# Masking causal scores in a grouped attention: a mask matmul on TensorE against an addition on VectorE

## The chip, the cores and the metric

The kernel runs on 1 core of one Trainium2 chip. The metric is device time in microseconds, shown as the median of 3 runs. Instructions run on five engines that each work through their own queue in order: PE (TensorE, matmuls; PEld are its weight loads), ACT (ScalarE), DVE (VectorE), POOL (GpSimd) and SP (SyncE, which issues DMAs). They are held together by semaphores: an instruction adds to one when it is done (`then_inc`), and an engine waits for a value (`wait_ge`).

## The reference

The program is four layers of attention and feed-forward on x of 8 batches x 128 tokens x 256 features. The change is in the last one, a grouped-query attention with a causal mask: 16 query heads of 128, 4 key and value heads.

```python
    h = rmsnorm(hidden, attn_norm_w)
    q = (h @ q_w.T).reshape(B, S, Hq, hd)
    k = (h @ k_w.T).reshape(B, S, Hkv, hd)
    v = (h @ v_w.T).reshape(B, S, Hkv, hd)
    q = rmsnorm(q, q_norm_w).transpose(0, 2, 1, 3)
    k = rmsnorm(k, k_norm_w).transpose(0, 2, 1, 3)
    ...
    q = apply_rope(q, cos, sin)
    k = apply_rope(k, cos, sin)
    k = jnp.repeat(k, n_rep, axis=1)
    v = jnp.repeat(v, n_rep, axis=1)
    scores = jnp.einsum('bhqd,bhkd->bhqk', q, k) * scale
    causal = jnp.tril(jnp.ones((S, S), bool))
    scores = jnp.where(causal[None, None], scores, jnp.finfo(scores.dtype).min)
    attn = jnp.einsum('bhqk,bhkd->bhqd', jax.nn.softmax(scores, axis=-1), v)
    attn = attn.transpose(0, 2, 1, 3).reshape(B, S, Hq * hd)
    hidden = hidden + attn @ o_w.T
```

## The kernel before

Stages follow one another on every engine; the grouped attention is the second half of `s47_pe`, `s47_act`, `s47_dve` and `s47_pool`, from about 895 to 1166 us. Its loop runs over m = 0 to 31: m = 4b + g, batch b and group g, a group being one key head and its four query heads. All tiles are float32 with 128 partitions (the tokens), four heads of 128 side by side (128x512, one bank of PSUM).

The order of work is written out by hand in each engine's loop over m, several groups being under way at once. In iteration m:

- PE (lines 2040 to 2068): `scores(m+1)`, `queries(m+3)` (projection, line 1916), `turn_probs(m)` (transposes, line 1922), `output(m-1)` (line 1967), `turn_queries(m+2)` (line 1922), then by g: 0 the keys of the next batch (line 1897), 2 the turning of those keys (`turn_keys`, line 1922), 3 the values (line 1904); last `weigh(m)` (probabilities by values, line 1958).
- ACT (lines 2228 to 2245): `copy_probs(m)` (line 2184), `exps(m+1)` (line 2175, four activations, each with an accumulator read; the scale is a pointer to the queries' norm, the bias a pointer to minus the maximum times that norm), `query_squares(m+3)` (line 2143), `copy_queries(m+2)` (line 2168); by g: 0 the squares of the last batch's output (line 2189) and of the next keys, 2 the copy of the turned keys (line 2164).
- DVE (lines 2515 to 2536): `copy_out(m-1)` (line 2458), at g = 0 the copy of the values (line 2439), `maxima(m+1)` (maximum, line 2443, and bias, line 2447), at g = 1 `normalise` (line 2470), `rotate_queries(m+3)` (lines 2403, 2405, 2419), `divide(m+1)` (lines 2451 and 2453), at g = 0 `hidden` (lines 2464 and 2466). At g = 2 it does `rotate_keys` (lines 2403, 2405, 2427, 2432) and the division ahead of the rotation of the queries.
- POOL raises the sums of squares to the power -1/2 (lines 2560 and 2564).

In the first iterations the engines also finish the last batches of the low-rank layer and of the memory attention (the parts `first`, `second`, `third`, `early`, `middle`, `late`).

The scores of two groups lie in the PSUM banks 4 and 2 in turn. The causal mask is 0 or -1e30, read from DRAM to `h_ca` (128x128); `tables` (lines 2290 to 2298, run once at m = 9 of the loop before) copies it four times side by side into `h_cm` as bfloat16. PE starts each group's scores with the identity times that mask and adds the four heads' products on top:

```python
pe.matmul(P[:, bank, :], idb[:, :], h_cm.rearrange("p j t -> p (j t)"), start=True, stop=False)   # line 1942
```

The maximum (DVE) and the exponentials (ACT) both read the masked scores in PSUM; PE may write a bank again when the exponentials of the group two before have ended (`h_exp`, line 1941).

Of the kernel before, what the change touches and what calls it, by code (L numbers as in the profile page):

```python
# [21 lines left out]
BF16 = mybir.dt.bfloat16  # L22
# [3 lines left out]
ALU = mybir.AluOpType  # L26
ACT = mybir.ActivationFunctionType
AX = mybir.AxisListType

B, T, D = 8, 128, 256  # L30
# [41 lines left out]
def build(nc, x, ctx, ctxT, mask, maskT, kvmask, a_wqT, a_wkT, a_wvT, a_bq, a_bk, a_bv, a_sel,  # L72
# [5 lines left out]
    with ex:  # L78
        def sb(name, shape, dt=F32):
            return ex.enter_context(nc.sbuf_tensor(name, shape, dt))  # L80
# [4 lines left out]
        P = ex.enter_context(nc.psum_tensor("P", [128, 8, 512], F32))  # L85
# [7 lines left out]
        idb = sb("idb", [128, 128], BF16)  # L93
# [1545 lines left out]
        fr2 = Arena(big2)  # L1639

        def heads3(at):
            return big3[:, at:at + 512].rearrange("p (j t) -> p j t", j=4)
# [27 lines left out]
        h_an, h_fn = fr2.view([128, D]), fr2.view([128, D])  # L1670
        h_qw, h_kw, h_c, h_sn, h_ca = (fr2.view([128, 128]) for _ in range(5))
        h_Cq, h_Sq, h_Ck, h_Sk = (fr2.view([128, 128]) for _ in range(4))
        h_cm = fr2.view([128, 4, T], BF16)
        H2 = [fr2.view([128, D]) for _ in range(2)]
        h_hh = fr2.view([128, D])
        h_V = [fr2.view([128, 512]) for _ in range(2)]
# [2 lines left out]
        h_qTs, h_kr, h_kTs, h_pts, h_t1, h_t2, h_jq, h_jk = map(  # L1679
            heads3, (0, 512, 1024, 1536, 7424, 7936, 8448, 8960))  # L1680
        h_pr = [heads3(9472), heads3(9984)]
        h_ss, h_sv, h_sr = (sm.view([128, B]) for _ in range(3))
        h_qs, h_qv, h_rq = (sm.view([128, 4, 4]) for _ in range(3))
        h_ks, h_kv, h_rk = (sm.view([128, 4]) for _ in range(3))
        h_mx, h_bi, h_z, h_r = ([sm.view([128, 4]) for _ in range(2)] for _ in range(4))
# [10 lines left out]
        h_qss, h_kss, h_qT, h_kT, h_exp, h_PT, h_yss, i_lgT, i_sl, h_s0 = act_again = (  # L1696
            a_e, c_ss, c_qkT, c_exp, c_PT, d_h, b_lgT, b_cTs, b_h, a_ab)
        h_v0, h_r0, h_qve, h_rqs, h_kve, h_rks, h_yve, h_yrs, i_cc = pool_again = (
            a_qkf, a_vp, a_p, a_parts, a_cc, c_cb, c_ve, c_rs, a_rt)
        h_ld, h_ld2, h_lt, i_ld, i_z = map(sem, ("h_ld", "h_ld2", "h_lt", "i_ld", "i_z"))  # L1700
        CLEAR = 6

        def again(eng, sems):
# [58 lines left out]
        def s47_pe(pe, last_rows):  # L1762
# [172 lines left out]
            def scores(m):  # L1935
                bank = 4 - 2 * (m % 2)
                pe.wait_ge(h_qT, m + 1)
                if m % 4 == 0:
                    pe.wait_ge(h_kT, m // 4 + 1)
                if m >= 2:  # L1940
                    pe.wait_ge(h_exp, m - 1)
                pe.matmul(P[:, bank, :], idb[:, :], h_cm.rearrange("p j t -> p (j t)"), start=True, stop=False)
                for j in range(4):
                    t = pe.matmul(P[:, bank, j * T:j * T + T], h_qTs[:, j, :], h_kTs[:, m % 4, :], start=False,
                                  stop=(j == 3))
                t.then_inc(h_s, 1)

            def turn_probs(m):
# [83 lines left out]
                    turn_fed()  # L2032
                weigh4(m)
            pe.wait_ge(e_exp, NM)
            pe.wait_ge(h_tab, 2)
            scores(0)
            turn_queries(1)
            pe.wait_ge(h_ld2, 64)
            queries(2)
            for m in range(NM):  # L2040
                b, g = divmod(m, 4)
                if m + 1 < NM:
                    if m == 0:
                        pe.wait_ge(e_vs, NM)
                    scores(m + 1)
                if m + 3 < NM:
                    queries(m + 3)
                first(NM + m)
                if m == 0:
                    pe.wait_ge(e_oT, NM)  # L2050
                turn_probs(m)
                second(NM + m)
                if m == 0:
                    output4(LAST)
                if m == 1:
                    pe.wait_ge(e_x, B)
                if m > 0:
                    output(m - 1)
                if m + 2 < NM:
                    turn_queries(m + 2)  # L2060
                if b + 1 < B and g == 0:
                    keys(b + 1)
                if b + 1 < B and g == 2:
                    turn_keys(b + 1)
                if b + 1 < B and g == 3:
                    values(b + 1)
                third(NM + m)
                weigh(m)
            output(NM - 1)

        def s47_act(act, last_rows):
# [98 lines left out]
            def exps(m):  # L2170
                act.wait_ge(h_bias, m + 1)
                if m >= 2:
                    act.wait_ge(h_t, m - 1)
                for j in range(4):
                    t = act.activation(h_pr[m % 2][:, j, :], P[:, 4 - 2 * (m % 2), j * T:j * T + T], ACT.Exp,  # L2175
                                       bias=h_bi[m % 2][:, j:j + 1], scale=h_rq[:, m % 4, j:j + 1],
                                       accum_out=h_z[m % 2][:, j:j + 1])
                t.then_inc(h_exp, 1)
# [17 lines left out]
            for m in range(NM):  # L2196
# [22 lines left out]
                if m == 4:  # L2219
                    act.wait_ge(tb_pe, 4 * B)  # L2220
                    for i in range(B - FED):
                        act.activation(XNT[:, :, (FED + i) * T:(FED + i) * T + T],
                                       P[:, 6, i * D:i * D + D].rearrange("p (k t) -> p k t", k=KD),
                                       ACT.Copy).then_inc(tb_ev, 1)
            exps(0)
            copy_queries(1)
            query_squares(2)
            for m in range(NM):
                b, g = divmod(m, 4)
                exps_memory(NM + m)  # L2230
                copy_probs(m)
                if m + 1 < NM:
                    exps(m + 1)
                first(NM + m)
                second(NM + m)
                if m + 3 < NM:
                    query_squares(m + 3)
                if m + 2 < NM:
                    copy_queries(m + 2)
                if b > 0 and g == 0:  # L2240
                    out_squares(b - 1)
                if b + 1 < B and g == 0:
                    key_squares(b + 1)
                if b + 1 < B and g == 2:
                    copy_keys(b + 1)
            out_squares(B - 1)

        def s47_dve(dve, last_rows):
# [40 lines left out]

            def tables():  # L2290
                dve.wait_ge(h_lt, 112)
                dve.tensor_copy(h_cm, h_ca.rearrange("p (a t) -> p a t", a=1).broadcast_to([128, 4, T])).then_inc(h_tab, 1)
                for C, S, w in ((h_Cq, h_Sq, h_qw), (h_Ck, h_Sk, h_kw)):
                    dve.tensor_tensor(C, h_c, w, ALU.mult)
                    dve.tensor_tensor(S[:, 0:64], h_sn[:, 0:64], w[:, 64:128], ALU.mult)
                    t = dve.tensor_tensor(S[:, 64:128], h_sn[:, 64:128], w[:, 0:64], ALU.mult)
                t.then_inc(h_tab, 1)
                dve.wait_ge(h_tab, 2)

            def choose(b):  # L2300
                n = 9 * b
# [138 lines left out]

            def maxima(m):
                dve.wait_ge(h_s, m + 1)
                dve.tensor_reduce(h_mx[m % 2], P[:, 4 - 2 * (m % 2), :].rearrange("p (j t) -> p j t", j=4), AX.X,
                                  ALU.max, negate=True).then_inc(h_max, 1)
                dve.wait_ge(h_max, m + 1)
                dve.wait_ge(h_rqs, m + 1)
                dve.tensor_tensor(h_bi[m % 2], h_mx[m % 2], h_rq[:, m % 4, :], ALU.mult).then_inc(h_bias, 1)
# [32 lines left out]
            for m in range(NM):  # L2480
# [20 lines left out]
                if m == CLEAR + 3:  # L2501
                    tables()
# [7 lines left out]
                late(m)  # L2510
            copy_out4(LAST)
            maxima(0)
            divide(0)
            rotate_queries(2)
            for m in range(NM):
                b, g = divmod(m, 4)
                if m > 0:
                    copy_out(m - 1)
                if b > 0 and g == 0:
                    copy_values(b)  # L2520
                if m + 1 < NM:
                    maxima(m + 1)
                early(NM + m)
                if b > 0 and g == 1:
                    normalise(b - 1)
                if b + 1 < B and g == 2:
                    rotate_keys(b + 1)
                    divide(m + 1)
                if m + 3 < NM:
                    rotate_queries(m + 3)  # L2530
                if m + 1 < NM and not (b + 1 < B and g == 2):
                    divide(m + 1)
                middle(NM + m)
                if b > 0 and g == 0:
                    hidden(b - 1)
                late(NM + m)
# [344 lines left out]
        @block.tensor  # L2881
        def _(pe):
            s0_pe(pe)
            s1_pe(pe)
            s47_pe(pe, s23_pe(pe))
            s8_pe(pe)
# [75 lines left out]
```

## Time and profile before

| | us |
|---|---|
| Runs: median (lowest, highest) of 3 | 1280.46 (1277.91, 1283.02) |
| The profiled execution: its time | 1279.11 |
| The profiled execution: its span in the trace | 1277.3 |
| Busy over the span: PE, DVE, ACT, POOL | 1087.5, 705.4, 503.4, 319.8 |

The profile is one execution. A page gives busy times and the chain of work that ended last, followed back from the last instruction to what released each one. Windows give each engine's busy time in a stretch with the number of its instructions, and the granted clock of TensorE (1.00 is 2.4 GHz, 0.50 is 1.2 GHz). A timeline lists instructions in order: start, duration, engine, line, operation, output<-input, shape, count, and in brackets how long the engine stood idle before and what released it. Starts follow one another closer than the durations, since an engine begins an instruction while the last one is ending. All times in the trace count from the start of the span. Some matmul records are missing (16 of 32 of line 1942).

### The profile page before, as it was taken

Reading aid. Unit: us, or ns where it says so; the run is one execution under the profiler, and the core shown is the slowest. Engines: PE = TensorE matmul, PEld = TensorE weight load, DVE = VectorE, ACT = ScalarE, POOL = GpSimd, SP = SyncE. Lnnn points to the kernel's source line nnn. Section 1 sums busy time; section 2 is a strip of 40 time slices with the busy share of each in tenths; the row PEclk is TensorE's granted clock in tenths of the full one; section 3 lists DMA queues with packets and bytes.
Section 4 is the critical chain, followed back from the end, with each engine's and each line's share of the span. In section 5 each row is a group of like instructions: output and inputs, shape, how many; then the busy total and the mean of one; then the engine's idle time right before and its main releaser. Section 6 shows DMA issues by size and latency. Waiting matters only on the chain.

```text
span 1277.3 us, 20613 instructions
## 1 busy us (share of the span) xinstructions
PE 1087.5 (85%) x7154; PEld 835.0 (65%) x7170; DVE 705.4 (55%) x1700; ACT 503.4 (39%) x1785; POOL 319.8 (25%) x440
## 2 busy tenths in 40 slices
PE   1788887899997688889999999997779999997494
PEld 0354545789996456678888888885556666665373
DVE  5876766211222778864454555555566666663544
ACT  0154563233231456654333333332445555553121
POOL 5543310222322345520000000001121222220472
PEclk9998996799999699999999999998989999998697
DMA  6443305898884070000000000032000000000595
GB/s 190 118 134 96 102 28 166 308 327 322 314 327 153 2 264 2 2 28 2 19 1 1 1 1 1 1 100 66 1 1 5 5 5 5 5 5 12 170 318 191
DMA packets 59732, 121.31 MB, mean 95 GB/s; under 512 B 9050, under 2 KB 37482, under 8 KB 53714
## 3 DMA queue, kind: packets, MB, share of 16 engines
q1 hardware_dynamic: 52217, 106.62, 24.9%
q0 software_dynamic: 4416, 12.06, 2.8%
q10 hardware_dynamic: 2996, 1.32, 0.4%
q8 instruction: 58, 0.95, 0.3%
q14 instruction: 45, 0.36, 0.1%
HBM read 107.29 MB, written 12.49 MB: 94 GB/s over the span
## 4 chain that ended last, share of the span: by engine, by line
PE 61%; DVE 17%; issue 7%; ACT 6%; DMA 6%; POOL 2%; SPq 1%; ACTq 0%; DVEq 0%; POOLq 0%
PE P L856 6%; PE P L866 5%; PE P L1778 4%; PE P L1771 4%; PE P L1823 4%; PE P L1787 4%; ACT big L2175 3%; DVE small L480 2%; PE P L1916 2%; PE P L2694 2%; PE P L1796 2%; PE P L1811 2%; DMA big<-b_w 2%; PE P L1922 2%; PE P L341 2%
## 5 line engine op out<-in xcount | busy, mean ns | idle before, releaser
L139 POOL TENSOR_TENSOR lrs<-lve,mhalf 128x1 f32<-128x1 f32 x64 | 36.6, 573 | 366.0 <-DVE lve L130 333.9
L480 DVE TENSOR_REDUCE small<-P 128x2 f32<-128x512 f32 x128 | 83.6, 681 | 44.4 <-PE P L305 43.8
L895 ACT ACTIVATE big<-P,big 128x128 f32<-128x128 f32 x184 | 52.5, 368 | 127.4 <-PE P L856 127.4
L2086 ACT ACTIVATE big<-P,small 128x128 f32<-128x128 f32 x128 | 45.3, 366 | 145.1 <-DVE small L2264 145.1
L556 ACT ACTIVATE big<-P 128x512 f32<-128x512 f32 x128 | 72.0, 598 | 64.0 <-PE P L323 58.3
L856 PE MATMUL P<-big 128*128 128x128 f32 x736 | 89.0, 281 | 1.7 <-DMA big<-b_w 1.5
L856 PEld LDWEIGHTS P<-big 128*128 128x128 f32 x736 | 86.6, 197 | 3.0 <-DMA big<-b_w 2.6
L305 PE MATMUL P<-big 90*128 90x256 bf16 x256 | 56.2, 310 | 32.3 <-DMA big<-scr_qk 17.5
L866 PE MATMUL P<-big 128*128 128x256 f32 x368 | 83.1, 380 | 0.0
L2255 DVE COPY big<-P 128x512 f32<-128x512 f32 x32 | 22.1, 692 | 107.2 <-PE P L1787 107.2
L988 DVE COPY big<-P 128x256 f32<-128x256 f32 x23 | 9.8, 425 | 127.5 <-PE P L866 127.5
L2403 DVE TENSOR_TENSOR big<-P,big 128x512 f32<-128x512 f32 x40 | 27.6, 690 | 85.4 <-ACT big L2143 85.2
L866 PEld LDWEIGHTS P<-big 128*128 128x128 f32 x368 | 68.4, 191 | 8.2
L1967 PE MATMUL P<-big 128*128 128x256 f32 x256 | 63.7, 394 | 0.8 <-DVE big L2458 0.8
L1771 PE MATMUL P<-XNT,big 128*128 128x128 f32 x512 | 62.6, 276 | 0.0
L1778 PE MATMUL P<-CT,big 128*128 128x128 f32 x512 | 62.4, 275 | 0.0
L1916 PE MATMUL P<-big,XNT 128*128 128x512 f32 x128 | 61.4, 603 | 1.2 <-DVE big L2405 1.2
L305 PEld LDWEIGHTS P<-big 90*128 90x128 bf16 x256 | 20.9, 105 | 62.7 <-DVE small L480 29.2
L1922 PEld LDWEIGHTS P<-idf,big 128*128 128x128 f32 x288 | 35.4, 146 | 40.0 <-issue 22.9
L1823 PE MATMUL P<-big 128*128 128x256 f32 x256 | 60.6, 380 | 0.0
L1787 PE MATMUL P<-big,CT 128*128 128x512 f32 x128 | 60.2, 593 | 0.0
L1771 PEld LDWEIGHTS P<-XNT,big 128*128 128x128 f32 x512 | 59.7, 192 | 0.2 <-issue 0.2
(383 smaller groups left out, 2590.6 us busy)
## 6 DMA issues: line engine op xcount, KB each, us to landing
big<-b_w SPq DMA_DIRECT2D x23, 1028.0 KB
big<-b_w SPq DMA_DIRECT2D x23, 1024.0 KB
big<-scr_qk SPq DMA_DIRECT2D x96, 96.0 KB
big<-i_wgu SPq DMA_DIRECT2D x23, 352.0 KB
big<-moe_y SPq DMA_DIRECT2D x16, 256.0 KB, 4.2
big<-i_wd SPq DMA_DIRECT2D x23, 176.0 KB
scr_qk<-big SPq DMA_DIRECT2D x8, 384.0 KB
moe_x<-XN SPq DMA_DIRECT2D x16, 128.0 KB, 1.8
```

The costliest lines, as they stand in the source:

```text
L305: t = pe.matmul(P[:, h % 2, c * D:c * D + D], QS[n % 3][0:90, h, c * 128:c * 128 + 128], KS[n % 3][0:90, h, :], start=True, stop=True)
L480: dve.tensor_reduce(negM[:, h, :], P[:, h % 2, :].rearrange("p (c s) -> p c s", c=2), AX.X, ALU.max, negate=True).then_inc(a_max, 1)
L556: act.activation(ER[:, g % 8], P[:, second_bank(i), :].rearrange("p (c t) -> p c t", c=2), ACT.Exp).then_inc(a_e, 1)
L856: m = pe.matmul(P[:, 2 * (j % 2) + f // 4, f % 4 * 128:f % 4 * 128 + 128], w1x[j % 3][:, k * F0 + f * 128:k * F0 + f * 128 + 128], xgT[j % ...
L866: m = pe.matmul(P[:, 6 + j % 2, 0:D], hT[j % 2][:, f, :], w2x[j % 3][:, f, :], start=(f == 0), stop=(f == FC - 1))
L1771: pe.matmul(P[:, 0, j * T:j * T + T], e_wqk[:, g, 0, k, j * 128:j * 128 + 128], XNT[:, k, b * T:b * T + T], start=(k == 0), stop=(k == KD ...
L1778: t = pe.matmul(P[:, 1, j * T:j * T + T], e_wqk[:, g, 1, k, j * 128:j * 128 + 128], CT[:, k, b * T:b * T + T], start=(k == 0), stop=(k == ...
L1787: t = pe.matmul(P[:, 2, :], CT[:, k, b * T:b * T + T], e_wvs[:, g, k, :], start=(k == 0), stop=(k == KD - 1))
L1823: t = pe.matmul(P[:, 7, 0:D], e_o[:, j, :], e_wos[:, 4 * g + j, :], start=(g == 0 and j == 0), stop=(g == 3 and j == 3))
L1916: t = pe.matmul(P[:, 0, :], XNT[:, k, b * T:b * T + T], h_wqs[:, g, k, :], start=(k == 0), stop=(k == KD - 1))
L1922: t = pe.transpose(P[:, bank, j * T:j * T + T], src[:, j, :], idf[:, :])
L1967: t = pe.matmul(P[:, 7, 0:D], h_o[:, j, :], h_wos[:, 4 * g + j, :], start=(g == 0 and j == 0), stop=(g == 3 and j == 3))
```

## The change

The mask matmul goes; the score matmuls each write their own quarter of the bank (`start=True`). DVE adds `h_ca`, broadcast over the four heads, while it takes the scores from PSUM to a new SBUF tile `h_sm` (two of them, in the place of the queries and keys of the attention before), waits for that to end, and takes the maximum from `h_sm`. The exponentials read `h_sm`. PE may write a bank again when DVE's masking of the group two before is done (`h_sma`); DVE may write an `h_sm` again when the exponentials of two before have ended. The bfloat16 copy of the mask and PE's wait for it go.

```diff
-        h_cm = fr2.view([128, 4, T], BF16)
+        h_sm = [heads3(2304), heads3(2816)]
...
@@ scores (PE)
                 if m >= 2:
-                    pe.wait_ge(h_exp, m - 1)
-                pe.matmul(P[:, bank, :], idb[:, :], h_cm.rearrange("p j t -> p (j t)"), start=True, stop=False)
+                    pe.wait_ge(h_sma, m - 1)
                 for j in range(4):
-                    t = pe.matmul(P[:, bank, j * T:j * T + T], h_qTs[:, j, :], h_kTs[:, m % 4, :], start=False,
-                                  stop=(j == 3))
+                    t = pe.matmul(P[:, bank, j * T:j * T + T], h_qTs[:, j, :], h_kTs[:, m % 4, :], start=True,
+                                  stop=True)
...
             pe.wait_ge(e_exp, NM)
-            pe.wait_ge(h_tab, 2)
             scores(0)
@@ exps (ACT)
-                    t = act.activation(h_pr[m % 2][:, j, :], P[:, 4 - 2 * (m % 2), j * T:j * T + T], ACT.Exp,
+                    t = act.activation(h_pr[m % 2][:, j, :], h_sm[m % 2][:, j, :], ACT.Exp,
@@ tables (DVE)
-                dve.tensor_copy(h_cm, h_ca.rearrange("p (a t) -> p a t", a=1).broadcast_to([128, 4, T])).then_inc(h_tab, 1)
...
-                dve.wait_ge(h_tab, 2)
+                dve.wait_ge(h_tab, 1)
@@ maxima (DVE)
                 dve.wait_ge(h_s, m + 1)
-                dve.tensor_reduce(h_mx[m % 2], P[:, 4 - 2 * (m % 2), :].rearrange("p (j t) -> p j t", j=4), AX.X,
-                                  ALU.max, negate=True).then_inc(h_max, 1)
+                if m >= 2:
+                    dve.wait_ge(h_exp, m - 1)
+                dve.tensor_tensor(h_sm[m % 2], P[:, 4 - 2 * (m % 2), :].rearrange("p (j t) -> p j t", j=4),
+                                  h_ca.rearrange("p (a t) -> p a t", a=1).broadcast_to([128, 4, T]),
+                                  ALU.add).then_inc(h_sma, 1)
+                dve.wait_ge(h_sma, m + 1)
+                dve.tensor_reduce(h_mx[m % 2], h_sm[m % 2], AX.X, ALU.max, negate=True).then_inc(h_max, 1)
```

## Rows read from the trace of the kernel before

**Rows 1.** The page, its part on the chain of work that ended last, by engine.

```profile
PE 61%; DVE 17%; issue 7%; ACT 6%; DMA 6%; POOL 2%; SPq 1%; ACTq 0%; DVEq 0%; POOLq 0%
```

**Rows 2.** Window of the whole stage: length, busy us by engine, clock, DMA share, GB/s.

```profile
895.00:1166.00 271.00, 237.06 (x1070) 156.85 (x1086) 174.15 (x397) 140.65 (x653) 57.41 (x97) 0.98 0.01 4
```

**Rows 3.** Timeline of PE, batches in the middle of the stage.

```profile
1007.15 1.05 PE L1944 MATMUL P<-big 128*128 128x128 f32 x8 [0.39 <-issue]
...
1071.48 1.05 PE L1944 MATMUL P<-big 128*128 128x128 f32 x8 [0.39 <-issue]
...
1079.27 0.38 PE L1942 MATMUL P<-big,idb 128*128 128x512 bf16 x1
1079.48 1.05 PE L1944 MATMUL P<-big 128*128 128x128 f32 x8
1080.38 1.88 PE L1916 MATMUL P<-big,XNT 128*128 128x512 f32 x4
1082.10 0.60 PE L1922 MATMUL P<-idf,big 128*128 128x128 f32 x4
...
1101.73 0.66 PE L1922 MATMUL P<-idf,big 128*128 128x128 f32 x4 [0.64 <-DVE big L2432]
...
1135.82 1.05 PE L1944 MATMUL P<-big 128*128 128x128 f32 x8 [0.40 <-issue]
```

**Rows 4.** Timeline of DVE, one of these batches.

```profile
1082.87 0.16 DVE L2447 TENSOR_TENSOR small<-small 128x4 f32<-128x4 f32 x1
1086.15 0.69 DVE L2403 TENSOR_TENSOR big<-P,big 128x512 f32<-128x512 f32 x1 [3.12 <-ACT big L2143]
...
1088.96 0.42 DVE L2464 TENSOR_TENSOR big<-P,XN 128x256 f32<-128x256 f32 x1
...
1089.76 0.68 DVE L2458 COPY big<-P 128x512 f32<-128x512 f32 x1
...
1096.05 0.69 DVE L2419 TENSOR_TENSOR big<-big 128x512 f32<-128x512 f32 x1
...
1098.08 0.68 DVE L2443 TENSOR_REDUCE small<-P 128x4 f32<-128x512 f32 x1
1098.79 0.16 DVE L2447 TENSOR_TENSOR small<-small 128x4 f32<-128x4 f32 x1
1098.87 0.69 DVE L2403 TENSOR_TENSOR big<-P,big 128x512 f32<-128x512 f32 x1
```

**Rows 5.** Timeline of ACT, the same batch.

```profile
1070.51 0.65 ACT L2164 ACTIVATE big<-P 128x512 f32<-128x512 f32 x1
...
1082.73 0.60 ACT L2184 ACTIVATE big<-P 128x512 f32<-128x512 f32 x1 [4.13 <-PE P L1922]
1083.22 0.45 ACT L2175 ACTIVATE big<-P,small 128x128 f32<-128x128 f32 x1
...
1084.96 0.29 ACT L2143 ACTIVATE big<-P 128x128 f32<-128x128 f32 x1
```

**Rows 6.** Timeline of ACT: exponentials elsewhere, from PSUM and from SBUF.

```profile
768.80 0.37 ACT L2086 ACTIVATE big<-P,small 128x128 f32<-128x128 f32 x1
769.05 0.21 ACT L2086 ACTIVATION_READ_ACCUMULATOR big<-P,small 128x1 f32 x1
...
914.50 0.40 ACT L2107 ACTIVATE big<-big,small 128x128 f32<-128x128 f32 x1 [1.41 <-DVE small L2393]
914.80 0.18 ACT L2107 ACTIVATION_READ_ACCUMULATOR big<-big,small 128x1 f32 x1
```

**Rows 7.** Timeline of DVE in the stage before, around the copy of the mask.

```profile
663.02 0.69 DVE L2255 COPY big<-P 128x512 f32<-128x512 f32 x1 [3.29 <-PE P L1787]
663.63 0.42 DVE L2292 CAST big<-big 128x512 bf16<-128x512 f32 x1
```

**Rows 8.** Two windows of five us; columns as in rows 2.

```profile
944.00:949.00 5.00, 1.51 (x8) 0.70 (x6) 3.24 (x9) 2.51 (x10) 0.55 (x1) 0.86 0.00 0
949.00:954.00 5.00, 4.62 (x14) 3.83 (x15) 2.41 (x6) 1.64 (x10) 1.27 (x2) 0.50 0.02 5
```

More of the change, by code:

```diff
@@ L1699, in build @@
             a_qkf, a_vp, a_p, a_parts, a_cc, c_cb, c_ve, c_rs, a_rt)
-        h_ld, h_ld2, h_lt, i_ld, i_z = map(sem, ("h_ld", "h_ld2", "h_lt", "i_ld", "i_z"))
+        h_ld, h_ld2, h_lt, i_ld, i_z, h_sma = map(sem, ("h_ld", "h_ld2", "h_lt", "i_ld", "i_z", "h_sma"))
         CLEAR = 6
```

## The prediction, made before the changed kernel was run

> **What bounds the kernel now.** I read the chain that ended last first: PE holds 61% of it, DVE 17%, ACT 6% [rows 1]. That is over the whole program, and the change touches one stage, the grouped attention, from about 895 to 1166 us. There PE is busy 237 us of 271 at a granted clock of 0.98, DVE 174 and ACT 141 [rows 2]. No engine is full: PE has 34 us of gaps, DVE 97. So the question is not which engine is the bound but which loop of work closes through three of them.
>
> The timeline of one batch (four groups) answers it. Call the four iterations of the loop over m by g = m mod 4. The score matmuls of g = 3 come at 1007.15, and in the same pattern three times more (the second of them at 1071.48) before they come at 1135.82 [rows 3]: four periods in 128.67 us, 32.17 each, 8.04 a group. PE comes close to filling it, but it is stopped: in g = 2 the turning of the keys waits 0.64 us for DVE's line 2432, and the scores of g = 3 stand 0.39 us [rows 3], behind ACT's copy of those keys. DVE meanwhile stands 3.12 us in g = 0 until ACT has the squares of the next queries [rows 4]. So DVE idles at one place and is late at another; work added to it is free only where it falls before such an idle stretch and nobody needs what comes after it.
>
> **What goes.** On PE, per group, the mask matmul: it starts at 1079.27 and the first score matmul follows at 1079.48, so it holds PE for 0.21 us, though its row says 0.38 [rows 3]. 32 of them are 6.7 us of PE's time, an upper bound; its weights are one more load, beside the matmuls. After an idle PE the score matmuls may have to show their own first weight load in its place: the lower bound is 0. Also gone is the one cast of the mask, 0.42 us on DVE; DVE had just stood 3.29 us waiting for PE there [rows 7], so PE is what hides it: it counts 0, and at most 0.4 without that cover. The scores of group m now wait for the masked copy of m-2 and not for its exponentials; that comes earlier, and no PE stop is put down to the exponentials, so it counts 0.
>
> **What comes, on DVE.** Per group one tensor_tensor, PSUM and a broadcast table in, SBUF out, 128x512. Line 2403 is the same form: 0.69 us [rows 4]. The reduce must wait for its end; the reduce's own reader, line 2447, starts 0.71 us after a reduce of 0.68, a handover of 0.03 [rows 4]. So the step is 0.72 us. The bounds are 0.61 (the start-to-start after a DVE instruction of this size that nobody waits for, 663.02 to 663.63 [rows 7]) and 0.75, another handover. 32 steps are 23 us of DVE. The wait for the exponentials of m-2 in front of it costs nothing: DVE has itself waited for them in the division of the iteration before. The reduce reads SBUF now. Line 2419, both operands in SBUF, takes 0.69, as line 2403 from PSUM does [rows 4], so I leave the reduce at its 0.68. The Trainium skill ("VectorE: DVE Perf Modes", section on the TRN2 errata) gives VectorE a fixed term of 120 cycles from PSUM and 58 from SBUF; by it the reduce would be an estimated 65 ns shorter, 0.2 us per batch in the loop below, some 1.6 us in all.
>
> **What changes on ACT.** The four exponentials of a group read SBUF. From the start of an exponential to that of its accumulator read it is 0.25 us at line 2086 (PSUM) and 0.30 at line 2107 (SBUF), both 128x128 with a bias pointer [rows 6]. I take 0.05 each, 0.20 a group: 1.74 becomes 1.94. Line 2175 has a scale pointer too, which may hide some of it: bounds 0 and 0.07.
>
> **The sum over one batch.** Step by step, start to start, from the timeline [rows 3 to 5], a DVE copy at 0.61 [rows 7], in the changed kernel:
> g = 3: scores 0.90 (1079.48 to 1080.38), queries 1.72, turning the probabilities until ACT copies them 0.63, that copy 0.49, exponentials 1.94, squares until DVE rotates 1.19 (1084.96 to 1086.15), rotation and division 2.81 (to 1088.96): 9.68.
> g = 0: copy out 0.61, copy of the values 0.61, masking, maximum and bias until ACT starts 0.72 + 0.71 + 0.16 + 0.03 = 1.62, exponentials 1.94, 1.19, 2.81, the residual (lines 2464 and 2466) 0.80: 9.58.
> g = 1: 0.61 + 1.62 + 1.94 + 1.19 + 2.81 = 8.17.
> g = 2: copy out 0.61, masking and maximum until the keys are rotated 0.72 + 0.79 (1098.08 to 1098.87) = 1.51, rotation until PE turns the keys 2.86 (to 1101.73), until ACT copies them 0.66 + 0.03, copy until the next scores 0.76 (1070.51 to 1071.27, which is 1071.48 less the 0.21 of the mask matmul): 6.43.
> Together 33.86 us against 32.17: **1.69 us more per batch**. By the old terms the same loop is 33.86 + 0.21 - 3 x 0.20 - 3 x 0.72 = 31.31, so today it is not the one that binds; in g = 0 and 1 ACT starts the exponentials when it has copied the probabilities (1083.22 is 0.49 after 1082.73), that is, when PE has come round. The slack of 0.86 is what swallows part of the 2.55 added. In the changed kernel the bias is what comes last before the exponentials of g = 0 and 1.
>
> Four batches are this clean. In the first ones DVE also carries work of the stages before, and the last has no keys to make; I take 1.69 there too. All eight: 13.5 us. The bounds: with exponentials at no cost and the masking at 0.61 the loop gives 1.69 - 0.60 - 3 x 0.11 = 0.76 a batch; and in the four other batches an iteration may take anything from nothing to the whole 0.92. So the sum lies between 4 x 0.76 = 3.0 and 4 x 1.69 + 16 x 0.92 = 21.5 us, the middle the likelier since both ends want every term at its end.
>
> The sum is against the profiled execution, 1277.3 us of span and 1279.11 in all; the median of the three runs, 1280.46, lies 1.35 above it. 1280.46 + 13.5 = **1294.0 us**. About 0.5% (6.4 us) is what a measurement of this kernel can tell from no change.
>
> **The rivals.**
> A. PE is the bound and DVE's idle time takes the new step. For it: PE is the fullest engine, DVE has 97 us idle [rows 2], some of it in waits of 3 us in each batch [rows 4]. Then 32 x 0.21 = 6.7 us go: 1273.8, faster. It decides if the bias of g = 0 and 1 is still ready before ACT has copied the probabilities, which needs 0.72 us of slack; the timeline leaves about 0.15 (line 2447 ends at 1083.03, the exponentials start at 1083.22 [rows 4, 5]). 0.06.
> B. ACT's reads from SBUF cost nothing beside a scale pointer. The loop loses 0.60: 33.26, 1.09 a batch, 8.7 us: 1289.2. For it: the scale pointer already lengthens these rows, 0.45 [rows 5] against 0.37 at line 2086 [rows 6]. Against it: nothing shows that the two overlap. 0.18.
> C. PE's longer gaps cost it the clock. Its idle time grows by 1.69 + 4 x 0.21 = 2.53 us a batch. Between 944 and 949 us PE was busy 1.51 us of 5, and from 949 to 954 it ran at a granted 0.50 (1.2 GHz) with 4.62 us busy [rows 8]: some 2.3 us lost. One such dip per batch would be 18 us on top: 1312. It decides once a gap grows to about that size. Against it: 2.53 us spread over the gaps of a batch leaves each of them well short of the 3.5 us that PE was idle in those five. The Trainium skill ("TensorE: Matmul & The Clock Gate", the section on HAM oscillation) says that idle gaps of TensorE in a loop can put it back to the low clock each time round, and speaks for this rival. 0.07.
> D. B holds, and the four unclean batches absorb the step in DVE's waits: 4 x 1.09 = 4.4 us, 1284.9, within 0.5%. For it: DVE was busy only 3.24 us between 944 and 949 [rows 8], so there is room. Against it: in such stretches the chain runs through DVE as often as through PE. 0.11.
> The forecast has the rest, 0.58.
>
> **How the numbers follow.** Slower by over 0.5%: forecast, B and C, 0.83. Same: D, 0.11. Faster: A, 0.06. The range leaves out A, C and the outer tails of the bounds: from 1284.5, which takes in D, to 1303, where the unclean batches cost almost the full step.
>
> **What would show it.** In the changed profile: no rows of line 1942; 32 new DVE rows of 0.69 us and the reduce 0.72 us behind each; the exponentials some 0.05 us longer each; a period of 33.9 us between the same instructions of two batches; ACT waiting for line 2447 in g = 0 and 1, where now it waits for PE only; PE's granted clock still 0.98. A period of 32.2 or less would break the loop argument; exponentials of unchanged length with a period of 33.3 would be B; more slices with a clock of 0.5 between 960 and 1150 would be C.

## The result, and the profile after

The changed kernel takes **1300.0 us** (median of 5 runs, 1296.77 to 1301.74) against 1280.97 for the kernel before on the same chip (5 runs, 1277.91 to 1283.02): a ratio of 1.0132 [1.0109, 1.0155], so slower by some 17 us (the two medians stand 19.0 apart). The forecast was 1294.0, in a range of 1284.5 to 1303.

The profiled execution took 1301.74 us with a span of 1299.9, 22.6 longer than that of before. I cut both spans at the first score matmul of the attention and at DVE's copy of the gates behind it. The stage between them went from 895.26 to 1179.9 us before and goes from 887.28 to 1190.1 now: 284.6 becomes 302.8, **18.2 us more**. The stages ahead of it are 8 us shorter; over the profiles of all thirteen runs, with either way of masking, they take anything from 884.9 to 895.3 us. What follows is 12.4 longer, 109.8 against 97.4; run c2 below shows that this is not the change.

The page, its chain by engine; DVE has taken 3% of the chain, PE has lost 2% [rows 1]:

```profile
PE 59%; DVE 20%; ACT 7%; issue 7%; DMA 4%; POOL 1%; SPq 1%; ACTq 0%; DVEq 0%; POOLq 0%
```

The window of 271 us that answers to rows 2, and four windows in which the clock fell, two in iteration 0 and two near the end of the stage (columns as in rows 2):

```profile
887.00:1158.00 271.00, 228.75 (x1007) 147.05 (x1006) 185.75 (x408) 140.11 (x630) 55.91 (x93) 0.97 0.01 4
895.00:900.00 5.00, 4.31 (x10) 1.93 (x10) 2.55 (x6) 0.42 (x1) 0.15 (x1) 0.66 0.00 0
900.00:905.00 5.00, 2.51 (x7) 2.17 (x8) 0.37 (x1) 3.76 (x19) 0.23 (x2) 0.72 0.00 0
1162.00:1167.00 5.00, 4.30 (x13) 3.51 (x14) 3.01 (x7) 2.53 (x10) 0.74 (x2) 0.50 0.08 26
1172.00:1177.00 5.00, 2.82 (x10) 1.88 (x10) 1.47 (x3) 2.19 (x9) 0.00 (x0) 0.83 0.01 3
```

PE is busy 229 us of 271 instead of 237, DVE 186 instead of 174: less work on the fullest engine, and yet a longer stage.

The timeline of PE, from g = 2 of one batch to g = 3 of the next:

```profile
1107.66 0.66 PE L1922 MATMUL P<-idf,big 128*128 128x128 f32 x4 [1.35 <-DVE big L2429]
1108.15 1.02 PE L1957 MATMUL P<-big 128*128 128x512 f32 x2
1109.05 1.13 PE L1943 MATMUL P<-big 128*128 128x128 f32 x8
1110.01 1.88 PE L1916 MATMUL P<-big,XNT 128*128 128x512 f32 x4
...
1125.12 1.16 PE L1943 MATMUL P<-big 128*128 128x128 f32 x8 [0.19 <-ACT big L2166]
...
1129.06 0.63 PE L1922 MATMUL P<-idf,big 128*128 128x128 f32 x4 [1.03 <-DVE big L2460]
...
1134.02 1.16 PE L1943 MATMUL P<-big 128*128 128x128 f32 x8 [1.31 <-ACT big L2166]
...
1142.70 1.13 PE L1943 MATMUL P<-big 128*128 128x128 f32 x8
```

The score matmuls of g = 3 come at 1008.09, 1041.74, 1075.40, 1109.05 and 1142.70: four batches in 134.61 us, **33.65 each** instead of 32.17. PE stands 1.35 us ahead of the turning of the keys (0.64 before [rows 3]), 1.03 ahead of g = 1's probabilities and 1.31 ahead of the scores behind them. These are places where the kernel before stood too, for 0.32 and 0.93 us:

```profile
1090.59 0.63 PE L1922 MATMUL P<-idf,big 128*128 128x128 f32 x4 [0.32 <-DVE big L2458]
1095.17 0.39 PE L1942 MATMUL P<-big,idb 128*128 128x512 bf16 x1 [0.93 <-ACT big L2168]
```

So the three waits of PE per batch have grown from 1.89 us to 3.69. The score matmuls take 1.13 where 1.05 stood, and 0.96 us pass to the queries instead of 0.90. In the clean batches it is 0.97 to 1.00 in three groups of four and 0.89 in the fourth; with the mask matmul in front (before, e8) it is 0.89 in every group. I read this, with no run of its own for it, as the first score matmul's own weight load, which shows where PE has just waited and the mask matmul no longer stands in front.

DVE and ACT in the same batch:

```profile
1110.32 0.68 DVE L2460 COPY big<-P 128x512 f32<-128x512 f32 x1
1110.92 0.68 DVE L2442 TENSOR_TENSOR big<-P,big 128x512 f32<-128x512 f32 x1
1111.64 0.69 DVE L2446 TENSOR_REDUCE small<-big 128x4 f32<-128x512 f32 x1
1112.36 0.16 DVE L2449 TENSOR_TENSOR small<-small 128x4 f32<-128x4 f32 x1
...
1115.91 0.69 DVE L2400 TENSOR_TENSOR big<-P,big 128x512 f32<-128x512 f32 x1 [3.39 <-ACT big L2141]
```

```profile
1112.86 0.48 ACT L2173 ACTIVATE big<-big,small 128x128 f32<-128x128 f32 x1
...
1114.77 0.26 ACT L2141 ACTIVATE big<-P 128x128 f32<-128x128 f32 x1
...
1120.22 0.60 ACT L2182 ACTIVATE big<-P 128x512 f32<-128x512 f32 x1 [3.86 <-PE P L1922]
1121.56 0.50 ACT L2173 ACTIVATE big<-big,small 128x128 f32<-128x128 f32 x1 [0.74 <-DVE small L2449]
1122.05 0.48 ACT L2173 ACTIVATE big<-big,small 128x128 f32<-128x128 f32 x1
```

The masking (line 2442) is in every group, the maximum 0.72 us behind it, the bias 0.72 behind that. In g = 0 ACT has copied the probabilities and stands 0.74 us for the bias, where before it started its exponentials at once [rows 5].

To see where the 18.2 us lie I cut the stage in three: the **head**, up to the score matmuls of m = 12; the four **clean** batches, m = 12 to 28; the **tail**, from there to the gates. (The head is three batches, the tail the last one with what drains behind it.) The experiments are in the same table.

| kernel | head | clean (one batch) | tail | stage |
|---|---|---|---|---|
| before | 111.9 | 128.7 (32.17) | 44.1 | 284.6 |
| after | 120.8 | 134.6 (33.65) | 47.4 | 302.8 |
| e1, no mask | 111.5 | 127.6 (31.91) | 44.8 | 283.9 |
| e2, DVE step only | 120.4 | 133.6 (33.39) | 46.1 | 300.0 |
| e3, step twice | 126.4 | 148.2 (37.05) | 48.4 | 323.0 |
| e4, after, fillers in m = 0 | 117.5 | 134.6 (33.65) | 47.0 | 299.1 |
| e5, after, residual later | 120.0 | 131.5 (32.86) | 47.9 | 299.4 |
| e6, before, residual later | 111.0 | 126.6 (31.66) | 44.2 | 281.9 |
| e7, e3 with fillers | 126.5 | 144.9 (36.23) | 51.9 | 323.3 |
| e8, e2 and ACT from SBUF | 121.7 | 135.2 (33.79) | 44.8 | 301.6 |
| e9, e6 with fillers | 108.7 | 126.7 (31.67) | 42.2 | 277.6 |

The head grows by 8.9 us, the clean part by 5.9, the tail by 3.3. The largest single growth in the head is iteration 0: from the scores of m = 1 to those of m = 2 it was 13.28 us (899.99 to 913.27) and is 16.62 (892.84 to 909.46). PE in it, before and after:

```profile
899.77 0.38 PE L1942 MATMUL P<-big,idb 128*128 128x512 bf16 x1 [1.30 <-ACT big L2168]
...
902.19 1.95 PE L1916 MATMUL P<-big,XNT 128*128 128x512 f32 x4 [1.15 <-DVE big L2405]
...
907.61 0.41 PE L1830 MATMUL P<-idf,XN 128*128 128x128 f32 x2 [2.81 <-ACT XNT L2098]
907.86 1.89 PE L1823 MATMUL P<-big 128*128 128x256 f32 x8
```

```profile
892.84 1.13 PE L1943 MATMUL P<-big 128*128 128x128 f32 x8 [2.34 <-ACT big L2166]
895.24 3.61 PE L1916 MATMUL P<-big,XNT 128*128 128x512 f32 x4 [1.27 <-DVE big L2402]
...
902.49 0.66 PE L1830 MATMUL P<-idf,XN 128*128 128x128 f32 x2 [2.94 <-ACT XNT L2096]
902.94 3.22 PE L1823 MATMUL P<-big 128*128 128x256 f32 x8
```

Three gaps stood close together already. The first has grown from 1.30 to 2.34 us, and behind it the queries take 3.61 us for the same work that took 1.95, and line 1823 takes 3.22 instead of 1.89. The granted clock of those ten us is 0.66 and 0.72 (above), where 1.00 was granted before.

The tail, in the kernel before, the changed one and e8:

```profile
1135.82:1179.89 44.07, 37.06 (x184) 27.98 (x184) 18.20 (x39) 17.51 (x68) 4.14 (x9) 0.92 0.03 9
1142.70:1190.11 47.41, 38.82 (x183) 28.80 (x182) 21.46 (x44) 18.27 (x68) 4.57 (x9) 0.88 0.03 8
1146.05:1190.83 44.78, 36.29 (x186) 26.88 (x184) 21.26 (x44) 18.29 (x68) 4.36 (x9) 0.95 0.03 9
```

The mean clocks of 0.92, 0.88 and 0.95 stand for some 7, 11 and 4 us at 1.2 GHz.

### The profile page after: what moved, and what is told of

Read it like the earlier page. It is cut to its first block, busy times and chain, and to the rows that moved or that the text cites. A ratio compares the mean times of both kernels' runs of the same rounds, so it can differ in the third digit from the quotient of the medians.

```text
span 1299.9 us, 20625 instructions
## 1 busy us (share of the span) xinstructions
PE 1091.6 (84%) x7138; PEld 832.9 (64%) x7138; DVE 725.9 (56%) x1731; ACT 509.9 (39%) x1785; POOL 320.4 (25%) x440
## 4 chain that ended last, share of the span: by engine, by line
PE 59%; DVE 20%; ACT 7%; issue 7%; DMA 4%; POOL 1%; SPq 1%; ACTq 0%; DVEq 0%; POOLq 0%
PE P L856 6%; PE P L866 6%; PE P L1778 4%; PE P L1823 4%; PE P L1771 4%; PE P L1787 4%; ACT big L2173 3%; PE P L2696 2%; DVE small L480 2%; PE P L1796 2%; PE P L1811 2%; DVE big L2402 2%; ACT big L2141 2%; PE P L1916 2%; PE P L341 2%
## 5 line engine op out<-in xcount | busy, mean ns | idle before, releaser
L139 POOL TENSOR_TENSOR lrs<-lve,mhalf 128x1 f32<-128x1 f32 x64 | 36.6, 573 | 364.9 <-DVE lve L130 323.9
L866 PE MATMUL P<-big 128*128 128x256 f32 x368 | 83.1, 379 | 0.0
L1922 PE MATMUL P<-idf,big 128*128 128x128 f32 x288 | 46.8, 289 | 26.2 <-DVE big L2460 15.5
L2173 ACT ACTIVATE big<-big,small 128x128 f32<-128x128 f32 x128 | 61.5, 482 | 13.9 <-DVE small L2449 11.9
L1966 PE MATMUL P<-big 128*128 128x256 f32 x256 | 65.3, 401 | 0.8 <-DVE big L2460 0.8
L1823 PE MATMUL P<-big 128*128 128x256 f32 x256 | 61.9, 386 | 0.0
```

Source lines behind the costliest of these rows:

```text
L866: m = pe.matmul(P[:, 6 + j % 2, 0:D], hT[j % 2][:, f, :], w2x[j % 3][:, f, :], start=(f == 0), stop=(f == FC - 1))
L1823: t = pe.matmul(P[:, 7, 0:D], e_o[:, j, :], e_wos[:, 4 * g + j, :], start=(g == 0 and j == 0), stop=(g == 3 and j == 3))
L1922: t = pe.transpose(P[:, bank, j * T:j * T + T], src[:, j, :], idf[:, :])
L1966: t = pe.matmul(P[:, 7, 0:D], h_o[:, j, :], h_wos[:, 4 * g + j, :], start=(g == 0 and j == 0), stop=(g == 3 and j == 3))
L2173: t = act.activation(h_pr[m % 2][:, j, :], h_sm[m % 2][:, j, :], ACT.Exp, bias=h_bi[m % 2][:, j:j + 1], scale=h_rq[:, m % 4, j:j + 1], acc ...
```

## The experiments

Theory: a loop of PE, ACT and DVE binds the stage and DVE's step is on it three times per batch; what the loop does not account for is TensorE's clock, lost in m = 0, where the kernel before keeps it, and for longer than before in the tail. Rivals: DVE's step is not the cost but ACT's read or the way PE now writes the bank; the rest of the growth is the step itself, in busier batches; the whole is a run's chance.

Between variants I go by the lengths of the stage's parts, one profile of each. The two kernels that were profiled twice repeat them within 0.3 us, while the intervals of the whole times of neighbouring variants (c2, e2, e4, e5, e8) overlap. Those times come from three chips, each with the kernel before beside it.

**c1, the kernel before again; c2, the changed kernel again.**

> The kernel before, unchanged, for a second profile. The profiled execution of the changed kernel is 22.6 us longer in span than that of before; of this 18.2 us lie in the stage of the grouped attention (from its first score matmul to the gates of the last stage), 12.4 us in the last stage, where DMA moved some 245 GB/s against 315, and 8 us are given back before the stage. Theory (the last and the first stages vary from one execution to the next and have nothing to do with the change): this profile has the grouped attention at 284.6 us within 1, periods of 32.17 us, while the stages before and after differ from the first profile of before by several us. Rival (the last stage is slower because of the change): the last stage here takes 97.4 us within 1 again, and 109.8 in the second profile of the changed kernel.

> The changed kernel, unchanged, for a second profile and more rounds. Theory: 1.2% to 1.5% slower, grouped attention at 302.8 us within 1, periods of 33.65; the last stage anywhere from 97 to 110 us. Rival: the last stage at 109.8 within 1 again.

c1 took 1274.21 us. c2: ratio 1.0135 [1.0101, 1.0170]. The stages last 284.9 and 302.9 us (884.89 to 1187.8 in c2), within 0.3 us of the first executions, and so do their parts (c2: 120.9, 134.6, 47.5). The window behind the stage, of the first execution after, then of c1, then of c2:

```profile
1190.10:1299.90 109.80, 65.74 (x308) 46.40 (x308) 46.55 (x136) 15.69 (x48) 44.96 (x47) 0.80 0.63 198
```

```profile
1174.30:1272.40 98.10, 61.89 (x309) 44.83 (x308) 47.38 (x136) 15.40 (x48) 45.05 (x47) 0.81 0.71 221
```

```profile
1187.80:1286.80 99.00, 63.01 (x308) 45.55 (x308) 47.25 (x136) 15.38 (x48) 44.94 (x47) 0.79 0.70 219
```

With the change in it the last stage takes 99.0, as without it; in the first execution its transfers ran at 198 GB/s. So 18 us are to be explained, and they lie in the grouped attention.

**e1, no mask at all.** Leaves out the causal mask, so it computes full attention; PE loses the mask matmul and nobody gets anything in its place.

```diff
-                pe.matmul(P[:, bank, :], idb[:, :], h_cm.rearrange("p j t -> p (j t)"), start=True, stop=False)
-                    t = pe.matmul(..., start=False, stop=(j == 3))
+                    t = pe.matmul(..., start=True, stop=True)
```

> The kernel before with the mask matmul taken out and nothing in its place (the causal mask is left out). It prices PE's side alone. Theory (a loop through three engines): the loop of before passes the score matmuls twice in a batch, so the period falls from 32.17 by 2 x 0.21 to 31.75 us, 3.4 us over the eight batches. Rival (PE is the bound): 0.84 a batch, 31.33 us, 6.7 in all. Rival (after an idle PE the first weight load shows in its place): under 0.25 a batch, under 2 us.

Ratio 1.0000 [0.9987, 1.0013]; stage 283.9, a period of 31.91, that is 0.26 less per batch where two full passes (0.42) were expected; the rival of the weight load, under 0.25, comes nearer. All that could be won by taking the mask off PE is about 1 us. A part of the reason is in a group behind a pause of PE:

```profile
1031.24 1.13 PE L1943 MATMUL P<-big 128*128 128x128 f32 x8 [0.20 <-issue]
1032.20 1.88 PE L1916 MATMUL P<-big,XNT 128*128 128x512 f32 x4
```

The score matmuls hold PE for 0.96 us, not 0.90 [rows 3]: part of the 0.21 us goes there, by the reading above into the first weight load. And PE's wait for DVE ahead of g = 1's probabilities grows from 0.32 to 0.61 us (1082.18 in e1), so PE only comes earlier to where it stands. e1 also writes the bank as the changed kernel does, each quarter with `start=True`, and loses nothing: that rival falls.

**e2, DVE's step alone.** The kernel before, with its mask matmul, and ACT still reading PSUM; DVE adds the mask once more into `h_sm` and takes the maximum there.

```diff
+                if m >= 2:
+                    dve.wait_ge(h_exp, m - 1)
+                dve.tensor_tensor(h_sm[m % 2], P[...], h_ca...broadcast_to([128, 4, T]), ALU.add).then_inc(h_sma, 1)
+                dve.wait_ge(h_sma, m + 1)
-                dve.tensor_reduce(h_mx[m % 2], P[...], AX.X, ALU.max, negate=True).then_inc(h_max, 1)
+                dve.tensor_reduce(h_mx[m % 2], h_sm[m % 2], AX.X, ALU.max, negate=True).then_inc(h_max, 1)
```

> The kernel before with DVE's new step added and nothing else: the mask matmul stays, DVE adds the mask a second time into an SBUF tile and takes the maximum from there, the exponentials still read PSUM (the maximum is the same). Theory (DVE's step and ACT's slower reads both lie on the loop): the period of the changed kernel, 33.65, plus 0.21 for the mask matmul, less 3 x 0.19 for the exponentials: 33.3 us, 1.1 a batch; in all 12 to 15 us slower than before. Rival A (DVE's idle time takes the step): no slower than before, period 32.2. Rival (all of the loss is DVE's, ACT's reads cost nothing): the same 17 us or more as the changed kernel.

Ratio 1.0114 [1.0091, 1.0137]; stage 300.0 (15.1 more than c1), period 33.39: 1.22 more per batch. The step alone carries most of the loss, with the mask matmul and ACT's reads as they were.

**e8, e2 with ACT's reads from SBUF.** The step from e2 to the changed kernel in two halves: e8 has both the mask matmul and the SBUF reads.

```diff
-                    t = act.activation(h_pr[m % 2][:, j, :], P[:, 4 - 2 * (m % 2), j * T:j * T + T], ACT.Exp,
+                    t = act.activation(h_pr[m % 2][:, j, :], h_sm[m % 2][:, j, :], ACT.Exp,
```

> The changed kernel with the mask matmul kept: PE adds the mask, DVE adds it again on the way to SBUF, the exponentials read SBUF. Against the changed kernel it prices the mask matmul, against the DVE step alone it prices ACT's reads. Theory (PE's 0.21 is not hidden where the loop passes the scores, ACT's 0.18 a group counts three times): 3 x 0.18 = 0.5 us a batch over the DVE step alone, period 33.39 + 0.5 = 33.9, and 0.1 to 0.25 over the changed kernel; in all 18 to 21 us slower than before. Rival (ACT's reads do not matter beside the DVE step): period 33.4.

Ratio 1.0141 [1.0112, 1.0171]; period 33.79. ACT's reads cost 0.40 us per batch over e2, and the mask matmul is worth 0.14 (33.79 to 33.65), with PE's earlier leave to write a bank and the dropped cast in the same step. The three parts of the change per batch are +1.22, +0.40 and -0.14, together the 1.48 measured. Its tail is 44.8 us, 2.6 below that of the changed kernel, though PE has 0.21 us more per group to do and all else is the same. It loses the clock there too, but for 4 us and not for 11 (the windows of the tail above). In iteration 0 it is the other way round: 18.29 us from the scores of m = 1 to those of m = 2, with the queries at 3.75 us, and a head of 121.7.

**e3, DVE's step twice.** The mask is added a second time, from SBUF to SBUF, with a wait of its own.

```diff
+                dve.tensor_tensor(h_sm[m % 2], h_sm[m % 2], h_ca...broadcast_to([128, 4, T]), ALU.add).then_inc(h_smb, 1)
+                dve.wait_ge(h_smb, m + 1)
```

> The changed kernel with the masking done twice: a second addition of the mask in place on the SBUF tile, each waiting for the one before. Theory (the loop passes maxima three times in a batch, in g = 0, 1 and 2, and not in g = 3): 3 x 0.73 = 2.2 us more per batch, period 33.65 + 2.2 = 35.85 us, some 18 to 20 us over the changed kernel. Rival (DVE's step lies on the path of every group): 4 x 0.73 = 2.9 a batch, period 36.6. Rival (it is the exponentials' SBUF reads that cost, not DVE): under 0.5 a batch.

Ratio 1.0310 [1.0280, 1.0340]; stage 323.0. The clean batches take 36.51, 37.22, 37.23 and 37.23 us, more than the 35.85 that the loop gives and more than the rival's 36.6. Windows of 3 us around the turning of the keys, and PE in them:

```profile
1126.00:1129.00 3.00, 0.92 (x9) 0.69 (x8) 2.90 (x7) 3.00 (x17) 0.19 (x1) 1.00 0.00 0
1129.00:1132.00 3.00, 3.00 (x12) 2.33 (x12) 2.82 (x7) 0.72 (x2) 1.32 (x2) 0.60 0.03 5
1132.00:1135.00 3.00, 3.00 (x11) 1.58 (x11) 2.17 (x4) 0.30 (x1) 0.00 (x0) 0.83 0.00 0
```

```profile
1128.43 0.66 PE L1922 MATMUL P<-idf,big 128*128 128x128 f32 x4 [2.08 <-DVE big L2429]
...
1129.98 1.92 PE L1943 MATMUL P<-big 128*128 128x128 f32 x8
```

Here the gap of 1.35 us has become 2.08, and the clock goes once per batch: the prediction's rival C, one step further on.

**e7, e3 with that gap filled.** Two matmuls whose result nobody reads stand ahead of the turning of the keys. (For e3 the expectation has a period of 37.38; the trace has 37.22 to 37.23.)

```diff
                 if b + 1 < B and g == 2:
+                    pe.wait_ge(h_PT, m + 1)
+                    for _ in range(2):
+                        pe.matmul(P[:, 5, :], XNT[:, 0, 0:T], h_wvs[:, 0, :], start=True, stop=True)
                     turn_keys(b + 1)
```

> The kernel with the masking done twice, and two matmuls of 512 columns that nobody reads put into PE's gap of 2.08 us ahead of the turning of the keys in g = 2, once per batch (1.7 us at full clock, so they fit). With the masking twice the period was 37.38 us where the loop gave 35.85, and behind that gap, in each batch, stood windows with a granted clock of 0.60 and 0.83. Theory (the 1.5 us beyond the loop are the clock): the clock stays at 1.00 and the period is 35.8 us within 0.2. Rival (DVE's step counts more than three times in a batch): period 37.2 to 37.5 still.

Ratio 1.0262 [1.0239, 1.0286]. The clean batches take 35.83, 36.27, 37.00 and 35.83; in the one of 37.00 the clock fell all the same (0.66 from 1115 to 1120 us). In the second, with the clock at 1.00, g = 1 takes 9.37 us where the first has 8.94: DVE arrives 0.43 us later, since g = 3's exponentials now wait for the bias too. So where e3 has 37.22, about 1 us is the clock's and at most 0.43 a fourth group on the loop. The stage as a whole did not get shorter, 323.3: the clean batches give back 3.3 us and the tail takes 3.5, with the clock at 0.50 from 1180 to 1185. This run supports the clock only within the batches. Its whole time is nearer to the kernel before than e3's, 1.0262 against 1.0310, on another chip and with intervals that just touch.

**e4, the changed kernel with the clock kept in m = 0.** One matmul that nobody reads is 0.86 us of PE; five of them lie in the gaps of m = 0, where PE would stand.

```diff
+            def filler(n):
+                for _ in range(n):
+                    pe.matmul(P[:, 1, :], XNT[:, 0, 0:T], h_wvs[:, 0, :], start=True, stop=True)
...
                     if m == 0:
                         pe.wait_ge(e_vs, NM)
+                        pe.wait_ge(h_vs, 1)
+                        filler(2)
                     scores(m + 1)
+                if m == 0:
+                    filler(1)
                 if m + 3 < NM:
                     queries(m + 3)
...
                 turn_probs(m)
+                if m == 0:
+                    filler(2)
```

> The changed kernel with five matmuls of 512 columns whose result nobody reads, put into the three longest gaps of PE in the iteration m = 0 (two ahead of the scores of group 1, one ahead of the queries of group 3, two ahead of the rows of the last batch), 0.86 us each at full clock. Theory (a longer gap of PE in m = 0 costs it the clock there, at windows with a granted 0.66 and 0.72, where before had 1.00): the clock stays at 1.00, the interval between the score matmuls of groups 1 and 2 falls from 16.6 to 13.7 us, the whole kernel by 2 to 3 us. Rival (the interval is longer because of DVE's and ACT's new work alone): nothing changes, or the fillers cost up to 1 us.

Ratio 1.0106 [1.0083, 1.0128]; stage 299.1, 3.7 less than after. From the scores of m = 1 to those of m = 2: 13.48 us, where the changed kernel had 16.62 and the kernel before 13.28. The two windows that stood at 0.66 and 0.72:

```profile
895.00:900.00 5.00, 4.38 (x16) 1.95 (x14) 2.26 (x7) 3.51 (x17) 0.98 (x2) 1.00 0.00 2
900.00:905.00 5.00, 4.33 (x14) 2.04 (x14) 2.70 (x6) 1.97 (x8) 0.29 (x1) 1.00 0.00 0
```

PE does more work in m = 0 and is through it 3.1 us sooner. The growth of that iteration was the clock, not the step itself; e2, whose iteration 0 takes 16.64 us, shows that the step alone is enough to bring the loss of the clock about. The head comes down to 117.5. It then has the clock at 1.2 GHz as long as the head before (one fall each, at 948 us), and is still 5.6 us longer, 1.9 a batch.

**e5, the residual later; e6, the same on the kernel before.** In g = 0 the residual (0.80 us) lies on the loop. `hidden` is moved to g = 1, behind the maxima; the squares of the output (ACT) and their mean (POOL) go to g = 1, `normalise` to g = 3, and two waits on ACT are for one batch earlier.

```diff
@@ DVE
+                if b > 0 and g == 1:
+                    hidden(b - 1)
                 early(NM + m)
-                if b > 0 and g == 1:
+                if b > 0 and g == 3:
                     normalise(b - 1)
...
-                if b > 0 and g == 0:
-                    hidden(b - 1)
```

> The changed kernel with the residual of a batch (0.80 us on DVE at the end of g = 0) moved behind the maximum of g = 1, ACT's squares of it to the end of g = 1, POOL's power with them, and the normalisation to g = 3. Theory (the loop runs through the end of g = 0 on DVE, and stands idle behind the maximum of g = 1): 0.80 us less a batch, period 32.85, 5 to 6 us in all against the changed kernel, so 11 to 12 slower than before. Rival (DVE has idle time anyway, so what is moved on it does not matter): period 33.65, no difference.

> The kernel before with the same move. Theory (its loop enters iteration 0 through PE but leaves it through the same squares, rotation, division and residual): period 32.17 - 0.80 = 31.4 us, 5 to 6 us faster than before, 0.4%, faster than both kernels. Rival (before is bound by PE, the residual hides beside it): period 32.17, no difference.

e5: ratio 1.0100 [1.0076, 1.0124], period 32.86, 0.79 less: the 0.80 taken off the loop comes back in full. e6: ratio 0.9990 [0.9972, 1.0007], no change that the whole time can tell; period 31.66, 0.51 less where 0.80 was expected. In the kernel before, PE stood 0.32 us ahead of g = 1's probabilities and 0.93 ahead of the scores behind them. In e6 0.23 (ahead of g = 1's output) and 0.48 are left of that: the 0.54 us that could be given back there are what came back, and the rest of the 0.80 meets PE's own work. The same edit is worth more in the kernel whose loop binds, as the loop argument says.

**e9, the kernel before with the residual later and the clock kept.** Fillers at m = 4 (three), m = 29 (three) and m = 31 (one), where the kernel before loses the clock too.

> The kernel before with the residual moved (period 31.66 instead of 32.17, and 2.8 us shorter in the stage) and with matmuls that nobody reads in PE's gaps at m = 4 (three), m = 29 (three) and m = 31 (one). Theory (two dips of the clock, at 949 to 958 us and 1155 to 1159 us in the profile of before, follow PE's gaps and cost some 2.2 and 1.7 us): the stage is 281.9 - 3.9 = 278 us, the whole kernel 5 to 7 us faster than before, beyond its interval. Rival (the clock falls there for another reason): dips stay, 281.9 us or up to 1 us more.

```profile
945.00:950.00 5.00, 4.78 (x20) 2.95 (x19) 1.66 (x4) 3.28 (x17) 1.26 (x2) 1.00 0.02 5
892.00:1169.00 277.00, 252.78 (x1166) 166.05 (x1165) 176.22 (x401) 144.07 (x664) 67.00 (x99) 1.00 0.02 5
```

Ratio **0.9948 [0.9929, 0.9968]**; stage 277.6, faster than both kernels. PE is busy 253 us of 277 at a mean clock of 1.00 (it falls only at 1166.5 us, in the last 3 us of the stage), where rows 8 show 0.86 and 0.50. Against e6 the fillers give 4.3 us, all of it in head and tail.

## Why the prediction was right, and where it was off

- **"which loop of work closes through three of them"**: right. Less work on PE and a longer stage, with PE waiting for DVE and ACT where the walk put it, is what the loop says and rival A (PE is the bound, 1273.8) excludes. e2 and e5 show it by adding to the loop and taking from it. What the walk says of the kernel before is less exact. It names two of PE's waits and leaves out those of 0.32 and 0.93 us in g = 1 and 2. Of the 0.39 us ahead of g = 3's scores, 0.21 is the mask matmul, whose record is missing there: its weight load is in the trace at 1103.40, the score matmuls at 1103.64, and e1, without it, shows 0.20 in the same place.
- **The DVE step, 0.72 on the loop three times**: right, 0.72 in each row, and +1.22 a batch in e2, where 3 x 0.72 less the slack of 0.86 is 1.30.
- **The reduce at its 0.68**: right, 0.69. The Trainium skill ("VectorE: DVE Perf Modes", section on the TRN2 errata) would have it an estimated 65 ns shorter from SBUF; the trace does not bear that out, 0.68 from PSUM and 0.69 from SBUF. The same table gives ScalarE 52 cycles more for a read from SBUF, an estimated 43 ns; there the trace agrees (next point).
- **Exponentials +0.05 each**: right, and rivals B and D, which want no cost there, fall. Start to start they went from 0.436 to 0.48. But the walk left "1.19" from the squares to the rotation and it is 1.14 (1114.77 to 1115.91), three times per batch; e8 shows 0.40 for ACT in all instead of 0.60.
- **The mask matmul, "0.21 us"**: mis-sized. It is worth 0.14 in the loop (e8), and 0.06 us of the difference is the longer way from the scores to the queries. The bound named this and the sum did not take it. It was far too small to matter.
- **"1.69 us more per batch"**: 1.48 measured, from the squares (-0.15), the exponentials (-0.07) and small terms.
- **"I take 1.69 there too"**, for the four batches of head and tail: this is the step that was off. It gives 6.8 us, and 12.2 were measured. In the head 3.3 of its 8.9 us are the clock lost in m = 0: e4 keeps it there and the head is 117.5 instead of 120.8. The 5.6 left are 1.9 a batch, the step in full and a little over. The tail grew by 3.3 us with some 4 us more at 1.2 GHz. Between e8 and the changed kernel 7 us more at 1.2 GHz go with a tail 2.6 us longer; by that rate an estimated 1.6 of the 3.3 are the clock and 1.7 the steps. Fillers in the tail of the changed kernel were not tried, so this part is a comparison and not shown. Together the steps cost about 13.3 us (5.6, 5.9 and 1.7), against a forecast of 13.5, and the clock about 5, for which the sum had no term.
- **Rival C**, the clock lost once per batch, at 0.07: it did not happen so; from 960 to 1160 us the clock stays at 1.00. The sum needed it in another form: the clock went in iteration 0, where PE already had three long gaps. The prediction looked for a grown gap in the clean batches alone, though rows 8 showed a dip in the head. And it set the gap that costs the clock beside 3.5 us of idle time; gaps of 2.34 and 1.27 us in m = 0, and of 2.08 in e3, were followed by a fall. The Trainium skill ("TensorE: Matmul & The Clock Gate", the section on HAM oscillation) speaks of gaps that take the clock each time round a loop; e3 and its 37.2 us show that this kernel is one step of 0.72 us away from it.
- **Rival D**, the unclean batches absorb the step: wrong, they grew by 12.2 us.
- The median of 1300.0 lies 6 us above the forecast; about 5 are the clock, the rest lies within what two measurements of one kernel differ by. That it fell into the range is in part luck: the upper end of 1303 was meant for unclean batches that pay the step in every iteration, and they did not.

## What to carry to other kernels

Where no engine is full, find the loop that closes through several of them and price an edit by how often it lies on it: here 0.21 us a group taken from the fullest engine was worth 0.14 to 0.26 a batch, and 0.72 us a group put on an engine idle a third of the time cost 1.22. Then look at the iterations that are not in the steady pattern, above all at places where TensorE already stands several times in a row: a gap that grew there by one us cost three. A few matmuls that nobody reads, put into such gaps, are cheap to try, on the kernel before the change as well.

## What was not expected of the hardware

- No single gap tells whether the clock goes: in iteration 0 pauses of 1.30, 1.15 and 2.81 us kept it at 1.00, pauses of 2.34, 1.27 and 2.94 within 12 us did not. In e3 the clean batches lost it with 2.08 us, in the changed kernel they kept it with 1.35. In e7 it fell in one batch of four with the fillers in.
- Filling a pause with useless work shortened iteration 0 by 3.1 us (e4), and head and tail of the kernel before, with the residual later, by 4.3 us (e9).
- The last stage, in the same code, took 109.8 us in one execution and 98.1 and 99.0 in two others, with 198 against 221 and 219 GB/s. A difference of two single executions can be half made of that, and only cutting the span at fixed instructions shows it.
